# Turning the first tile's query rows and rows with attention by transposing transfers instead of TensorE, with the early orders planned for it

## The chip, the cores and the metric

One core of one Trainium2 chip runs the kernel. The metric is device time in microseconds (us) of one execution, the median of several runs. The core has TensorE (PE; PEld is its weight load), VectorE (DVE), ScalarE (ACT), GpSimd (POOL) and the SyncE queue (SP), which issues all transfers here; the transfers are done by 16 DMA engines.

## The reference

Inputs: `x` of 4 x 1024 x 2048, 64 context keys of 2048 per batch, two gates, a weight of 2048 x 2048 and a bias, all f32.

```
x = x + tanh(g_xattn) * C(layernorm(x))
    C: a = q @ keys^T ; e = softmax(a) ; c = e @ keys
x = x + tanh(g_ffn) * (layernorm(x) @ W^T + bias)
    W = mean(|weight|, per output row) * sign(weight)
```

## The kernel before

The 4096 rows of `x` are 32 tiles of 128 rows. For each tile u:

- **Layernorm 1.** ACT sums the rows and their squares (`sum_rows1`, `square_rows1`; for the first two tiles DVE does it with `ln1_mean`), and POOL makes the scale. `direct_high_q` on ACT then writes the normalised rows as a high f16 part and `low_q` on DVE the f16 rest, both into a slot of `natural`. There are two halves (h = 0, 1) of 1024 columns per tile, and three slots for all that has to be transposed.
- **Turning.** What stands in a `natural` slot has its rows on partitions and has to be transposed for TensorE. Nearly all of it is done by a transposing transfer (`turn_block`, L426, a DMA_TRANSPOSE issued by SP), into `qt` for query rows, `ring_a` or `xn_b` for the rows with attention (called x1). For tile 0 alone, query rows and x1 rows are turned by TensorE in before: `turn_rows` (L2511) multiplies 2 x 8 blocks of 128 x 128 by the identity, part by part, into the two PSUM banks `turn_ps`; then ACT copies one part out and DVE the other (`take_q` L1026 and L1611, `take_x1` L1031 and L1616).
- **Attention.** `scores(u)` (L2553, 32 matmuls of 128 columns), a softmax over 64 keys (`max_logits`, `exp`, `split_probs`, `transpose_probs`, `copy_pt`), four `attend(u, n)` (L2569, two matmuls of 512 columns each), and four times `attention(u, n)` on DVE, which adds the result to the rows.
- **Layernorm 2**, with x1 again in two f16 parts.
- **Product with W.** The signs of the weight are made once, in 16 row blocks w: SP loads a block (`load_w`, four stage buffers), ACT takes signs (`sign`, L1057) and the sum of magnitudes (`sum_abs`, L1063), TensorE turns two blocks at a time (`turn_w(j)`, L2523), ACT and DVE copy them into `wsign` (`take_w(j)`, L1068 and L1754). The row means go through `spread_alpha`, `turn_alpha`, `take_alpha`. Tiles 0 to 3 are multiplied directly: `plain_block(t, n, q)` (L2589, 8 matmuls of 512 columns; q = 0 to 3 make one block of tile t and 512 outputs n). `plain_block(0, n, 0)` waits for both copies of `turn_w(2n+1)`. From tile 4 on, tiles go in 14 pairs through seven half-size products (L2621, `half_product`), with added rows `S1` to `S4`.

All five engines run a list of calls that is written out in the source, so each engine takes its instructions in that order and a late one holds up all behind it. Three tables fix what the lists must agree on: `PE_Q` and `PE_X1` (below which tile TensorE turns), `TURNS` (the order in which TensorE uses the two `turn_ps` banks, which ACT and DVE must have emptied) and `NAT` (the order in which `natural` slots are filled).

The waits that matter for the start:

```
plain_block, q == 0, t == 0:
    pe.wait_ge(out_act, turn("w", 2 * n + 1) + 1)
    pe.wait_ge(out_dve, turn("w", 2 * n + 1) + 1)
turn_w(j):   pe.wait_ge(w_signed, w + 1)      # w = 2j, 2j + 1
             wait_bank(h, "w", j)             # earlier copies out of turn_ps
turn_q:      sp.wait_ge(scores_ready, u)
turn_block:  sp.wait_ge(low_set, i + 1)
sum_rows1:   act.wait_ge(low_set, nat("q", u - 1, 1) + 1)
```

Of the kernel before, what the change touches and what calls it, by code (L numbers as in the profile page):

```python
# [14 lines left out]
def flamingo_gated_kernel(  # L15
# [52 lines left out]
    PE_Q, PE_X1 = 1, 1  # L68
# [3 lines left out]
    TURNS = [("k", 0, 0), ("q", 0, 0), ("q", 0, 1), ("k", 0, 1), ("w", 0, 0), ("w", 1, 0), ("x1", 0, 0),  # L72
              ("w", 2, 0), ("alpha", 0, 0), ("x1", 0, 1), ("w", 3, 0), ("w", 4, 0), ("w", 5, 0), ("alpha", 1, 0),
              ("w", 6, 0), ("w", 7, 0), ("alpha", 2, 0), ("alpha", 3, 0)]
# [82 lines left out]
    with ExitStack() as ctx:  # L157
# [240 lines left out]
        def _(sp):  # L398
# [73 lines left out]
            load_keys(0)  # L472
            load_w(0)
            load_w(1)
            load_gates()
            load_x(1)
            load_x(2)
            load_w(2)
            load_x(3)
            load_w(4)  # L480
            load_w(3)
            load_w(5)
            turn_q(1, 0)
            turn_q(1, 1)
            turn_q(2, 0)
            load_x(4)
            turn_q(2, 1)
            load_w(6)
            load_bias()
            load_w(7)  # L490
            turn_q(3, 0)
            turn_x1(1, 0)
            turn_q(3, 1)
# [4 lines left out]
            turn_q(4, 0)  # L498
            turn_x1(2, 0)
            turn_q(4, 1)  # L500
            turn_x1(2, 1)
            load_w(11)
            load_w(12)
            load_w(13)
            load_w(14)
            load_w(15)
            load_x(5)
# [7 lines left out]
            store(1)  # L515
            store(2)
            load_x(7)
            turn_q(6, 0)
            load_x(8)
            turn_a(0, "A11")  # L520
            turn_q(6, 1)
            turn_a(0, "A12")
            turn_a(0, "S3")
            turn_q(7, 0)
            store(3)
            turn_q(7, 1)
            load_x(9)
            turn_a(0, "S2")
            turn_a(0, "S1")
            turn_a(0, "A22")  # L530
            turn_q(8, 0)
            turn_q(8, 1)
            turn_a(0, "S4")
# [5 lines left out]
            load_x(10)  # L539
            turn_a(1, "S2")  # L540
            turn_q(9, 0)
            turn_q(9, 1)
            store(5)
            turn_a(1, "S1")
            load_x(11)
            turn_q(10, 0)
# [5 lines left out]
            turn_a(2, "A12")  # L552
            store(6)
            turn_q(11, 1)
            load_x(12)
# [63 lines left out]
            store(15)  # L619
            turn_a(6, "S2")  # L620
            turn_a(6, "A22")
            turn_a(6, "S1")
            load_x(21)
# [112 lines left out]
        def _(pool):  # L736
# [83 lines left out]
            mean_1(4)  # L820
            scale1(4)
            scale2(2)
            scale2(3)
            mean_1(5)
            scale1(5)
            scale2(4)
            mean_1(6)
# [6 lines left out]
            reduce_keys(1)  # L834
# [5 lines left out]
            rstd1(10)  # L840
            mean_1(11)
            scale2(8)
# [68 lines left out]
        def _(act):  # L911
# [176 lines left out]

            direct_high_q(0, 0)
            sign(0)  # L1090
            high_keys(0)
            direct_high_q(0, 1)
            tanh_gates()
            sign(1)
            sum_abs(0)
            take_keys(0)
            sum_abs(1)
            take_q(0, 0)
            direct_high_q(1, 0)
            take_q(0, 1)  # L1100
# [3 lines left out]
            sum_abs(2)  # L1104
# [3 lines left out]
            copy_pt(0)  # L1108
            sign(3)
            direct_high_q(2, 0)  # L1110
            sign(4)
            take_w(0)
            direct_high_q(2, 1)
            sign(5)
            exp(1)
            take_w(1)
            direct_high_x1(0, 0)
            copy_pt(1)
            sum_rows1(3)
# [2203 lines left out]
```

## Time and profile before

| what | value |
|---|---|
| runs, median (lowest to highest) | 985.3 us (984.62 to 986.54) |
| the profiled execution's own time | 985.79 us |
| its span, first to last instruction | 984.0 us |
| PE busy | 934.0 us (95%) |
| DVE busy | 840.8 us (85%) |
| ACT busy | 589.3 us (60%) |
| chain that ended last | PE 69%, DVE 10%, issue 7%, ACT 5% |
| mean granted TensorE clock | 0.988 |

A busy share is time in which the engine had an instruction in work, over the span. "Idle before" is the time an engine stood still ahead of an instruction, and "<-" names what it waited for. The chain that ended last is followed back from the last instruction to what released each step. The profiled time is 1.8 us above its span, and 0.5 us above the median.

### The profile page before, as it was taken

Reading aid. Unit: us, or ns where it says so; the run is one execution under the profiler, and the core shown is the slowest. Engines: PE = TensorE matmul, PEld = TensorE weight load, DVE = VectorE, ACT = ScalarE, POOL = GpSimd, SP = SyncE. Lnnn points to the kernel's source line nnn. Section 1 sums busy time; section 2 is a strip of 40 time slices with the busy share of each in tenths; the row PEclk is TensorE's granted clock in tenths of the full one; section 3 lists DMA queues with packets and bytes.
Section 4 is the critical chain, followed back from the end, with each engine's and each line's share of the span. In section 5 each row is a group of like instructions: output and inputs, shape, how many; then the busy total and the mean of one; then the engine's idle time right before and its main releaser. Section 6 shows DMA issues by size and latency. Waiting matters only on the chain.

```text
span 984.0 us, 14349 instructions
## 1 busy us (share of the span) xinstructions
PE 934.0 (95%) x5201; PEld 462.9 (47%) x5201; DVE 840.8 (85%) x1197; ACT 589.3 (60%) x655; POOL 134.9 (14%) x262
## 2 busy tenths in 40 slices
PE   1669999999999999999999999999999999999998
PEld 1445554444444444454444444444444445444443
DVE  6587799897888989899989979998989888889864
ACT  5999973856587573646657364745667464562320
POOL 0011020131001110203111220201102020111000
PEclk9779999999999999999999999999999999999999
DMA  9589747696897988787995959967797967765374
GB/s 332 181 233 229 225 128 199 179 202 112 185 218 154 217 158 221 150 177 168 217 239 97 242 121 237 196 144 202 165 230 125 240 137 152 196 128 102 65 177 186
DMA packets 365141, 178.66 MB, mean 182 GB/s; under 512 B 353424, under 2 KB 353424, under 8 KB 354448
## 3 DMA queue, kind: packets, MB, share of 16 engines
q1 hardware_dynamic: 365072, 177.76, 76.9%
q8 instruction: 41, 0.67, 0.3%
q14 instruction: 28, 0.23, 0.1%
HBM read 55.58 MB, written 33.55 MB: 91 GB/s over the span
## 4 chain that ended last, share of the span: by engine, by line
PE 69%; DVE 10%; issue 7%; ACT 5%; POOL 2%; DMA 2%; SPq 0%; ACTq 0%; DVEq 0%; POOLq 0%
PE y_ps L2621 53%; PE y_ps L2589 7%; PE c_ps L2569 5%; PE s_ps L2553 4%; DVE natural L1571 3%; ACT xn_q L952 1%; DVE xr L1656 1%; DMA xr<-in_x_dram 1%; ACT natural L933 1%; DMA ring_a<-natural 1%; ACT spare L1063 1%; DVE st L1661 1%; DVE snap_a L1689 0%; ACT xn_q L919 0%; DVE xr L1790 0%
## 5 line engine op out<-in xcount | busy, mean ns | idle before, releaser
L2621 PE MATMUL y_ps<-wsign,ring_a 128*128 128x512 fp8e4 x1792 | 400.6, 379 | 2.3 <-DMA ring_a<-natural 1.5
L2621 PEld LDWEIGHTS y_ps<-wsign,ring_a 128*128 128x128 f16 x1792 | 173.9, 98 | 209.8 <-DMA ring_a<-natural 2.8
L2621 PE MATMUL y_ps<-spare,ring_a 128*128 128x512 fp8e4 x896 | 202.8, 379 | 0.7 <-ACT snap_b L1087 0.7
L933 ACT ACTIVATE natural<-xn_a 128x1024 f16<-128x1024 f32 x76 | 79.5, 1053 | 109.2 <-DVE xn_a L1803 49.9
L2621 PEld LDWEIGHTS y_ps<-spare,ring_a 128*128 128x128 f16 x896 | 87.3, 98 | 105.8 <-issue 1.5
L952 ACT ACTIVATE xn_q<-xr,nm,r 128x1024 f32<-128x1024 f32 x62 | 76.8, 1238 | 68.7 <-POOL nm L791 34.3
L1571 DVE TENSOR_TENSOR natural<-xn_a,natural 128x1024 f16<-128x1024 f32 x78 | 94.7, 1216 | 10.9 <-ACT natural L933 10.9
L1571 DVE TENSOR_TENSOR natural<-xn_q,natural 128x1024 f16<-128x1024 f32 x64 | 78.1, 1220 | 25.3 <-ACT natural L933 25.0
L2621 PE MATMUL y_ps<-sg,ring_a 128*128 128x512 fp8e4 x448 | 99.4, 379 | 0.0
L1656 DVE SCALAR_TENSOR_TENSOR xr<-c_ps,coef,xr 128x512 f32<-128x512 f32 x104 | 77.6, 746 | 21.5 <-PE c_ps L2569 21.1
L2569 PE MATMUL c_ps<-kd,pt 128*128 128x512 f16 x256 | 79.7, 394 | 11.5 <-DVE xr L1656 8.6
L2589 PE MATMUL y_ps<-wsign,ring_a 128*128 128x512 fp8e4 x384 | 85.2, 379 | 0.6 <-DVE ring_a L1616 0.6
L1661 DVE BATCH_NORM_STATS2 st<-xr 128x6 f32<-128x512 f32 x104 | 72.2, 694 | 3.6
L1790 DVE TENSOR_TENSOR xr<-xr,bias_b 128x2048 f32<-128x2048 f32 x32 | 72.9, 2281 | 0.0
L784 POOL TENSOR_SCALAR mean<-sum 128x1 f32<-128x1 f32 x30 | 14.7, 489 | 415.9 <-ACT xn_q L919 398.8
L2621 PEld LDWEIGHTS y_ps<-sg,ring_a 128*128 128x128 f16 x448 | 43.6, 98 | 51.8
L927 ACT ACTIVATE xn_q<-xr,mean 128x2048 f16<-128x2048 f32 x30 | 59.9, 1997 | 12.9 <-POOL mean L784 12.7
L919 ACT ACTIVATE xn_q<-xr 128x2048 f16<-128x2048 f32 x30 | 57.2, 1907 | 17.4 <-DMA xr<-in_x_dram 12.0
L2553 PEld LDWEIGHTS s_ps<-kt,qt 128*128 128x128 f16 x1024 | 63.5, 102 | 8.2 <-ACT kt L1019 0.8
L933 ACT ACTIVATE natural<-xn_q 128x1024 f16<-128x1024 f32 x62 | 65.5, 1057 | 2.1 <-DMA qt<-natural 0.2
L2553 PE MATMUL s_ps<-kt,qt 128*128 128x128 f16 x1024 | 66.2, 226 | 0.6 <-ACT kt L1019 0.6
L1703 DVE TENSOR_TENSOR xr<-snap_a,xr 128x512 f32<-128x512 f32 x84 | 58.1, 692 | 2.9
(121 smaller groups left out, 1001.4 us busy)
## 6 DMA issues: line engine op xcount, KB each, us to landing
xr<-in_x_dram SPq DMA_DIRECT2D x32, 1024.0 KB, 6.2
out_dram<-xr SPq DMA_DIRECT2D x30, 1024.0 KB, 5.1
spare<-n_L_ffn_weight_real_dram SPq DMA_DIRECT2D x8, 1024.0 KB, 7.3
ctx_f<-in_ctx_dram SPq DMA_DIRECT2D x8, 512.0 KB, 6.6
xr<-n_L_ffn_weight_real_dram SPq DMA_DIRECT2D x4, 1024.0 KB, 5.0
ctx_f<-n_L_ffn_weight_real_dram SPq DMA_DIRECT2D x4, 1024.0 KB, 7.3
out_dram<-xr SPq DMA_DIRECT2D x8, 256.0 KB, 2.2
ring_a<-natural SPq DMA_TRANSPOSE x102, 4.5
```

What stands on the lines that cost most here:

```text
L927: nc.scalar.activation(junk, xr[:, u % RX, :], ACT.Square, bias=mean1[:, :], accum_out=sq1[:, :]).then_inc(sq1_set, 1)
L933: nc.scalar.activation(natural[:, i % RN, 0, :], src, ACT.Copy).then_inc(high_set, 1)
L952: nc.scalar.activation(xn_q[:, :], xr[:, u % RX, half(h)], ACT.Identity, bias=nm1[:, :], scale=r1[:, :]).then_inc(xn1_set, 1)
L1571: nc.vector.tensor_tensor(natural[:, i % RN, 1, :], src, natural[:, i % RN, 0, :], ALU.subtract).then_inc(low_set, 1)
L1656: nc.vector.scalar_tensor_tensor(out=xr[:, r, chunk(n)], in0=c_ps[:, :], scalar=coef[:, u % 2:u % 2 + 1], in1=xr[:, r, chunk(n)], op0=ALU. ...
L1661: nc.vector.bn_stats(st2[:, n, :], xr[:, r, chunk(n)]).then_inc(stats2, 1)
L1703: nc.vector.tensor_tensor(xr[:, r, chunk(m)], tmp, xr[:, r, chunk(m)], ALU.add).then_inc(y_added, 1)
L1790: nc.vector.tensor_tensor(xr[:, r, :], xr[:, r, :], bias_b[:, :], ALU.add).then_inc(x1b_set, 1)
L2553: last = nc.tensor.matmul(s_ps[:, 0:P], qt[:, k // HALF, part, k % HALF, :], kt[:, k, :], start=(k == 0 and part == 0), stop=(k == ND - 1 ...
L2569: last = nc.tensor.matmul(c_ps[:, :], pt[:, u % 2, :], kd[:, part, chunk(n)], start=(part == 0), stop=(part == 1))
L2589: last = nc.tensor.matmul(y_ps[:, j % 4, :], x1_block(t, k // HALF)[:, part, k % HALF, :], w8[:, k // 2, chunk(n), k % 2], start=(k == 0 a ...
L2621: last = nc.tensor.matmul(y_ps[:, BANKS[j] + n, :], ring_a[:, slot_a(p, j), part, k, :], RIGHT[j][:, k // 2, chunk(n), k % 2], start=(firs ...
```

## The change

Tile 0 is treated like all other tiles: `PE_Q` and `PE_X1` become 0, `turn_rows`, `take_q` and `take_x1` are called no more, and SP issues four more transposing transfers. The lists of all engines are written in another order as far as about tile 12 and at two places near tile 19. Early in the lists, the gates are loaded before the first weight block, `tanh_gates` is ACT's first call, the second tile's `ln1_mean` stands ahead of `low_keys`, and the bias is loaded earlier. Line numbers of the changed kernel are 3 higher on ACT, 1 lower on DVE and SP, 5 lower on PE.

```diff
-    PE_Q, PE_X1 = 1, 1
+    PE_Q, PE_X1 = 0, 0
-    TURNS = [("k", 0, 0), ("q", 0, 0), ("q", 0, 1), ("k", 0, 1), ("w", 0, 0), ("w", 1, 0), ("x1", 0, 0),
-              ("w", 2, 0), ("alpha", 0, 0), ("x1", 0, 1), ("w", 3, 0), ("w", 4, 0), ("w", 5, 0), ("alpha", 1, 0),
+    TURNS = [("k", 0, 0), ("k", 0, 1), ("w", 0, 0), ("w", 1, 0), ("w", 2, 0), ("alpha", 0, 0), ("w", 3, 0),
...
@@ ACT
             copy_pt(0)
+            take_w(0)
+            direct_high_q(2, 0)
+            sum_abs(2)
+            direct_high_q(2, 1)
             sign(3)
...
+            normalise2(1)
+            high_x1(1, 0)
             take_w(1)
...
@@ PE
             turn_maxima()
             turn_keys(0)
-            turn_rows("q", 0, 0)
-            turn_rows("q", 0, 1)
             turn_keys(1)
             scores(0)
...
             scores(1)
-            turn_w(1)
             transpose_probs(1)
             attend(1, 0)
-            turn_rows("x1", 0, 0)
             attend(1, 1)
             attend(1, 2)
             attend(1, 3)
+            turn_w(1)
+            scores(2)
+            transpose_probs(2)
             turn_w(2)
```

**TensorE, from tile 2's attention to the first product of tile 1.** Before (L2511 is the second half of tile 0's x1, L2523 turns weights, L2530 the row means, L2589 is the direct product, x8 for each call):

```order
L2530 MATMUL y_ps<-ident,snap_b 128x128 x4
L2511 MATMUL y_ps<-ident,natural 128x128 x16
L2560 MATMUL s_ps<-ident,prob 128x128
L2589 MATMUL y_ps<-wsign,ring_a 128x512 x24
L2569 MATMUL c_ps<-kd,pt 128x512 x2
L2589 MATMUL y_ps<-wsign,ring_a 128x512 x8
L2569 MATMUL c_ps<-kd,pt 128x512 x2
L2523 MATMUL y_ps<-ident,sg 128x128 x16
L2569 MATMUL c_ps<-kd,pt 128x512 x2
L2553 MATMUL s_ps<-kt,qt 128x128 x32
L2569 MATMUL c_ps<-kd,pt 128x512 x2
L2589 MATMUL y_ps<-wsign,ring_a 128x512 x48
```

Now, the same stretch, from `turn_w(2)` on:

```order
L2518 MATMUL y_ps<-ident,sg 128x128 x16
L2584 MATMUL y_ps<-wsign,ring_a 128x512 x8
L2564 MATMUL c_ps<-kd,pt 128x512 x2
L2584 MATMUL y_ps<-wsign,ring_a 128x512 x8
L2525 MATMUL y_ps<-ident,snap_b 128x128 x4
L2584 MATMUL y_ps<-wsign,ring_a 128x512 x8
L2564 MATMUL c_ps<-kd,pt 128x512 x2
L2584 MATMUL y_ps<-wsign,ring_a 128x512 x8
L2564 MATMUL c_ps<-kd,pt 128x512 x4
L2518 MATMUL y_ps<-ident,sg 128x128 x16
L2548 MATMUL s_ps<-kt,qt 128x128 x32
L2584 MATMUL y_ps<-wsign,ring_a 128x512 x32
```

The transposes of x1 are gone, `turn_w(2)` moved from ahead of `scores(2)` to just ahead of the first product, the row means moved into it, and `turn_w(3)` with `scores(3)` now stand behind all four attentions of tile 2.

**ScalarE, around the copy `take_w(1)` that the first product waits for.** Before (xn_q and natural together are one half of a tile's query rows, sg is a block's signs, ex the exponential):

```order
L952 ACTIVATE xn_q<-xr,nm,r 128x1024
L933 ACTIVATE natural<-xn_q 128x1024
L1057 ACTIVATE sg<-spare 128x8x2x128
L1068 COPY wsign<-y_ps 128x8x128
L952 ACTIVATE xn_q<-xr,nm,r 128x1024
L933 ACTIVATE natural<-xn_q 128x1024
L1057 ACTIVATE sg<-spare 128x8x2x128
L1036 ACTIVATE ex,sum_ex<-logits,neg_max,lscale 128x64
L1068 COPY wsign<-y_ps 128x8x128
```

Now, ending at the same copy:

```order
L1060 ACTIVATE sg<-spare 128x8x2x128
L930 ACTIVATE xn_q,sq1<-xr,mean1 128x2048
L941 ACTIVATE natural<-xr,nm2,r2 128x1024
L1060 ACTIVATE sg<-spare 128x8x2x128
L1066 ACTIVATE spare,abs_sum<-spare 128x2048
L955 ACTIVATE xn_q<-xr,nm1,r1 128x1024
L936 ACTIVATE natural<-xn_q 128x1024
L1039 ACTIVATE ex,sum_ex<-logits,neg_max,lscale 128x64
L1001 ACTIVATE xn_a<-xr,nm2,r2 128x2048
L936 ACTIVATE natural<-xn_a 128x1024
L1071 COPY wsign<-y_ps 128x8x128
```

Before, this copy follows the exponential of tile 1; now it follows that of tile 2, tile 1's second normalisation, a half of tile 3's queries and five magnitude sums (blocks 0 to 4).

**The SP queue at the start.** Before:

```order
L405 DMA xr<-in_x_dram 128x2048
L414 DMA ctx_f<-in_ctx_dram 64x2048 x2
L435 DMA spare<-in_L_ffn_weight_real_dram 128x2048 x2
L438 DMA gates<-in_g_xattn_dram 128x1
L439 DMA gates<-in_g_ffn_dram 128x1
L405 DMA xr<-in_x_dram 128x2048 x2
L435 DMA xr<-in_L_ffn_weight_real_dram 128x2048
L405 DMA xr<-in_x_dram 128x2048
L435 DMA spare<-in_L_ffn_weight_real_dram 128x2048
L435 DMA ctx_f<-in_L_ffn_weight_real_dram 128x2048
L435 DMA spare<-in_L_ffn_weight_real_dram 128x2048
L426 DMA_TRANSPOSE qt<-natural 128x16x128 x3
```

Now, from the first weight block on:

```order
L434 DMA spare<-in_L0_ffn_weight_real_dram 128x2048
L404 DMA xr<-in_x_dram 128x2048
L434 DMA spare<-in_L0_ffn_weight_real_dram 128x2048
L434 DMA xr<-in_L0_ffn_weight_real_dram 128x2048
L425 DMA_TRANSPOSE qt<-natural 128x16x128
L404 DMA xr<-in_x_dram 128x2048
L425 DMA_TRANSPOSE qt<-natural 128x16x128
L441 DMA bias_b<-in_L0_ffn_bias_dram 128x2048
L404 DMA xr<-in_x_dram 128x2048
L425 DMA_TRANSPOSE qt<-natural 128x16x128
```

The two transposing transfers of tile 0's queries now stand between loads, so that tiles 2 and 3, the bias and the later weight blocks are issued only after the waits of these transfers.

## Rows read from the trace of the kernel before

**Rows 1.** The profile's page, busy time by engine and one group of DVE.

```profile
PE 934.0 (95%) x5201; PEld 462.9 (47%) x5201; DVE 840.8 (85%) x1197; ACT 589.3 (60%) x655; POOL 134.9 (14%) x262
...
L1656 DVE SCALAR_TENSOR_TENSOR xr<-c_ps,coef,xr 128x512 f32<-128x512 f32 x104 | 77.6, 746 | 21.5 <-PE c_ps L2569 21.1
```

**Rows 2.** Busy time by stage: stretch, length, engines' busy us, clock, DMA share, GB/s.

```profile
0.00:80.00 80.00, 41.53 (x312) 28.29 (x313) 53.73 (x95) 66.07 (x66) 8.05 (x33) 0.85 0.80 246
...
200.00:300.00 100.00, 97.50 (x572) 48.78 (x571) 84.23 (x130) 67.92 (x84) 14.63 (x28) 1.00 0.81 175
```

**Rows 3.** Timeline of PE: start, length, instruction, idle before it and its releaser.

```profile
31.91 3.57 PE L2553 MATMUL s_ps<-kt,qt 128*128 128x128 f16 x32 [0.56 <-ACT kt L1019]
...
40.20 1.03 PE L2569 MATMUL c_ps<-kd,pt 128*128 128x512 f16 x2 [1.40 <-ACT pt L1043]
...
71.61 5.34 PE L2589 MATMUL y_ps<-wsign,ring_a 128*128 128x512 fp8e4 x24 [0.58 <-DVE ring_a L1616]
76.79 0.59 PE L2569 MATMUL c_ps<-kd,pt 128*128 128x512 f16 x2
...
80.83 1.95 PE L2553 MATMUL s_ps<-kt,qt 128*128 128x128 f16 x32
...
83.05 10.52 PE L2589 MATMUL y_ps<-wsign,ring_a 128*128 128x512 fp8e4 x48
...
152.35 0.66 PE L2530 MATMUL y_ps<-ident,snap_b 128*128 128x128 f32 x4 [0.64 <-DVE snap_b L1762]
```

**Rows 4.** Groups by line and shape, 0 to 80 us: what the change removes.

```profile
L2511 PE MATMUL y_ps<-ident,natural 128*128 128x128 f16 x64 | 6.7, 287 | 4.3 <-ACT kt L1019 2.2 <-DVE alpha_b L1768 1.2 <-ACT qt L1026 0.9
...
L1026 ACT COPY qt<-y_ps 128x1024 f16<-128x1024 f16 x2 | 2.0, 994 | 0.0
L1031 ACT COPY ring_a<-y_ps 128x1024 f16<-128x1024 f16 x2 | 2.0, 990 | 0.0
...
L1611 DVE COPY qt<-y_ps 128x1024 f16<-128x1024 f16 x2 | 1.4, 693 | 2.3 <-PE y_ps L2511 2.3
L1616 DVE COPY ring_a<-y_ps 128x1024 f16<-128x1024 f16 x2 | 1.4, 681 | 0.0
```

**Rows 5.** The query tile `qt`, 0 to 75 us: landing of its transposing transfers.

```profile
DMA to landing us min/median/max: 4.3/4.6/5.7
```

**Rows 6.** Timeline of DVE: second half of tile 0's queries, then tile 1's statistics.

```profile
20.19 1.23 DVE L1571 TENSOR_TENSOR natural<-xn_q,natural 128x1024 f16<-128x1024 f32 x1
...
21.67 2.46 DVE L1563 BATCH_NORM_STATS2 st<-xr 128x6 f32<-128x512 f32 x4
```

**Rows 7.** Timeline of ACT, 66 to 82 us: one of each kind.

```profile
66.93 2.09 ACT L998 ACTIVATE xn_a<-xr,nm,r 128x2048 f32<-128x2048 f32 x1 [1.14 <-POOL nm L780]
68.94 0.42 ACT L1036 ACTIVATE ex<-logits,neg_max,lscale 128x64 f32<-128x64 f32 x1
...
71.20 0.26 ACT L1043 COPY pt<-s_ps 128x128 f16<-128x128 f16 x1
71.36 1.25 ACT L952 ACTIVATE xn_q<-xr,nm,r 128x1024 f32<-128x1024 f32 x1
72.63 1.06 ACT L933 ACTIVATE natural<-xn_q 128x1024 f16<-128x1024 f32 x1
...
76.34 1.90 ACT L1057 ACTIVATE sg<-ctx_f 128x2048 fp8e4<-128x2048 f32 x1
78.14 1.89 ACT L919 ACTIVATE xn_q<-xr 128x2048 f16<-128x2048 f32 x1
...
80.04 1.89 ACT L1063 ACTIVATE spare<-spare 128x2048 f32<-128x2048 f32 x1
...
81.93 1.99 ACT L927 ACTIVATE xn_q<-xr,mean 128x2048 f16<-128x2048 f32 x1
```

**Rows 8.** Busy time by 5 us, columns as in rows 2: the granted clock at the start.

```profile
35.00:40.00 5.00, 1.88 (x22) 1.57 (x20) 1.51 (x9) 5.00 (x9) 0.25 (x1) 0.93 0.71 133
40.00:45.00 5.00, 3.10 (x6) 0.39 (x6) 2.89 (x4) 4.97 (x5) 0.95 (x3) 0.50 0.42 78
```

More of the change, by code:

```diff
@@ L1166, in _ @@
             sum_abs(14)
+            take_w(6)
             sign(15)
-            take_w(6)
+            take_w(7)
+            sum_rows1(5)
+            exp(4)
+            square_rows1(5)
             sum_abs(15)
-            sum_rows1(5)
-            take_w(7)
-            square_rows1(5)
+            copy_pt(4)
             normalise2(3)
@@ L1860, in _ @@
             attention(0, 1)
+            low_q(2, 0)
             attention(0, 2)
-            spread_alpha(0)
-            low_q(2, 0)
+            attention(0, 3)
+            low_q(2, 1)
             take_w(0)
-            attention(0, 3)
             max_logits(1)
+            scale_bias()
+            split_probs(1)
             rows_x1(0)
-            split_probs(1)
-            low_q(2, 1)
+            attention(1, 0)
+            attention(1, 1)
+            low_x1(0, 0)
+            attention(1, 2)
@@ L1897, in _ @@
+            low_x1(2, 0)
             add_bias(0)
-            split_probs(3)
+            low_x1(2, 1)
+            add_bias(1)
+            spread_alpha(5)
+            add_bias(2)
+            attention(3, 0)
+            spread_alpha(6)
             finish_y(0, 0)
-            spread_alpha(4)
+            take_w(4)
+            spread_alpha(7)
+            take_w(5)
             low_q(4, 0)
-            low_x1(2, 0)
+            attention(3, 1)
+            finish_y(1, 0)
             low_q(4, 1)
-            attention(3, 0)
@@ L1905, in _ @@
-            low_x1(2, 1)
-            attention(3, 1)
-            add_bias(1)
+            take_alpha(1)
+            spread_alpha(8)
+            spread_alpha(9)
+            finish_y(0, 1)
             attention(3, 2)
-            spread_alpha(5)
+            spread_alpha(10)
+            finish_y(1, 1)
+            finish_y(2, 0)
+            make_t1(0)
+            take_w(6)
+            make_t2(0)
+            attention(3, 3)
             max_logits(4)
             split_probs(4)
-            spread_alpha(6)
@@ L1943, in _ @@
             spread_alpha(14)
+            take_alpha(2)
+            finish_y(2, 1)
             spread_alpha(15)
+            attention(4, 0)
+            low_q(5, 0)
             finish_y(0, 2)
+            finish_y(1, 2)
+            attention(4, 1)
+            low_x1(3, 0)
             low_q(5, 1)
+            key_max(1)
+            finish_y(2, 2)
             take_alpha(3)
-            finish_y(1, 2)
-            finish_y(2, 2)
+            finish_y(0, 3)
             low_x1(3, 1)
-            finish_y(0, 3)
-            make_t1(1)
+            make_n4(0)
+            attention(4, 2)
             max_logits(5)
+            attention(4, 3)
             split_probs(5)
@@ L2216, in _ @@
             make_s4(6)
+            add_bias(17)
+            attention(18, 0)
+            attention(18, 1)
+            low_a(6, "A22")
             attention(18, 2)
@@ L2676, in _ @@
             attend(3, 0)
+            turn_w(4)
             plain_block(1, 1, 1)
             plain_block(1, 1, 2)
+            plain_block(1, 1, 3)
+            turn_w(5)
             attend(3, 1)
[L2680 to L2683 removed]
             plain_block(2, 0, 0)
             plain_block(2, 0, 1)
[L2686 to L2702 removed]
+            plain_block(2, 0, 2)
+            turn_alpha(1)
+            plain_block(2, 0, 3)
+            attend(3, 2)
+            plain_block(2, 1, 0)
+            plain_block(2, 1, 1)
+            plain_block(2, 1, 2)
+            plain_block(2, 1, 3)
+            turn_w(6)
+            plain_block(0, 2, 0)
+            plain_block(0, 2, 1)
+            attend(3, 3)
             plain_block(0, 2, 2)
+            scores(4)
+            turn_w(7)
             plain_block(0, 2, 3)
@@ L2735, in _ @@
             plain_block(3, 0, 2)
+            plain_block(3, 0, 3)
             attend(5, 3)
-            plain_block(3, 0, 3)
             plain_block(3, 1, 0)
@@ L2818, in _ @@
             half_product(1, 4, 0, 1)
-            scores(10)
             attend(9, 3)
@@ L2822, in _ @@
             half_product(1, 4, 1, 1)
+            scores(10)
             half_product(1, 5, 0, 0)
@@ L2834, in _ @@
             half_product(2, 0, 1, 0)
[L2835 removed]
+            scores(11)
+            attend(10, 1)
             half_product(2, 0, 1, 1)
             half_product(2, 1, 0, 0)
[L2838 to L2839 removed]
             half_product(2, 1, 0, 1)
@@ L2991, in _ @@
             half_product(5, 6, 1, 1)
+            scores(19)
+            transpose_probs(19)
             half_product(6, 0, 0, 0)
@@ L2994, in _ @@
             half_product(6, 0, 0, 1)
-            scores(19)
             attend(18, 1)
```

487 lines of the change are left out of this document (211 added, 276 removed), and 12 rows, old and new, of the table NAT.

## The prediction

> **What bounds the kernel now.** I read the busy times first: PE 934.0 of 984.0 us [rows 1], so the time is TensorE's work plus the 50 us in which it has none. The stages say where these lie: in the first 80 us PE is busy for 41.5, so 38.5 of the 50 are lost there, while ACT is busy for 66.1 of 80 [rows 2]. Of ACT's 14 idle us most lie ahead of the first rows' statistics, so in the rest of that stretch it hardly rests: the start is ACT's. Third, PE's own timeline: the first product of a tile with the weight starts at 71.61, that of tile 1 at 83.05 [rows 3], and behind it PE runs dense, with one wait of 0.64 at 152.35 for the last row means, which hang on ACT's last magnitude sums. The end therefore moves with two things: how much work PE has done by the time it runs dense, and the few waits after that.
>
> **What the change removes.** On PE 64 transposes, 6.7 us; on ACT four copies of 0.99, 4.0 us; on DVE four copies of 0.69, 2.7 us [rows 4]. PE's 6.7 us lie in the stretch in which it waits for others, mostly beside that waiting; they are worth at most what ACT and DVE let through. ACT's 4.0 us are the real offer. In their place stand four transposing transfers, 4.3 to 5.7 us from issue to landing [rows 5].
>
> **First scores.** They start at 31.91 behind ACT's second copy of keys [rows 3]. The calls on ACT ahead of that copy are the same as before, less two copies of 0.99 (the gates' tanh and `sum_abs(0)` only change places). So the copy comes 2.0 earlier, and the scores at 29.9. The second half of tile 0's queries must have landed by then. DVE finished it at 20.19 + 1.23 = 21.4; now `ln1_mean(1)`, whose statistics took 2.46 with another 0.3 to join them [rows 6], and the gates' 0.4 stand ahead of it: 24.6. With 4.6 us of landing that is 29.2. It just fits. At the bounds of [rows 5] the scores start between 29.9 and 30.4, if no load is in the way. I take 29.9: a gain of 2.0 so far.
>
> **From there to the first product: ACT's list.** `plain_block(0, 0, 0)` needs `take_w(1)` on ACT. In the new order that copy stands behind tile 2's exponential and a half of tile 3's queries. From the end of the key copy, 29.8 by the step above, ACT has ahead of it: three signs, three magnitude sums and two row sums (8 x 1.90 = 15.2), two squares (4.0), four query halves (1.25 + 1.06 each, 9.2), two halves of x1 at 1.25 (2.5), three exponentials with their read-out (about 0.6 each, 1.8), two copies of probabilities (0.5), the normalisation of tile 1 (2.1) and one high half (1.0), and two copies of weights at 0.99, the price of a copy of this shape [rows 4], 2.0. That is 38.3 [rows 7]: 68.1 if ACT never waits.
>
> It will wait. The sum over tile 2's rows waits for DVE's low half of q(1, 1) (1.23 [rows 6]): 1.3. The sum over tile 3's rows waits for q(2, 1)'s low half, which stands on DVE behind the last attention of tile 0: 0.7. Tile 2's exponential waits for its scores. DVE's four attentions of tile 1 (0.75 each [rows 1] and the statistics behind them) now have the two low halves of x1 between them, which eats the 2.0 us won above, so the scores come where they were, ending near 67: 1.7. Another 1.0 goes into smaller waits for POOL. Sum 4.7: `take_w(1)` is done at **72.8**. By the bounds (no wait, or twice these) it is 68.1 to 77.5; rows for these waits exist before only one by one, so I take the middle. `turn_w(2)` must follow that copy, having no bank before it, and the first product starts at about 74, against 71.61.
>
> **The next gate: sign(7).** PE's list puts `turn_w(3)` and `scores(3)` ahead of tile 1's product, and `turn_w(3)` needs the signs of block 7. Before, ACT had them at 76.34 + 1.90 = 78.2 [rows 7]. Now there stand between `take_w(1)` and that point: a magnitude sum, a copy of probabilities, a query half, a copy of weights, a high half, a sign, a row sum and the sign itself, 1.9 + 0.3 + 2.3 + 1.0 + 1.0 + 1.9 + 1.9 + 1.9 = 12.2. So the signs are ready at 85.0. With 0.5 for the second half of `turn_w(3)` and 1.95 for the scores [rows 3], tile 1's product starts at 87.4. Up to that start both orders have done the same work on PE, apart from the 64 transposes. So this is the lag: 87.4 - 83.05 = **4.3 us**.
>
> The mechanism in one sentence: the four copies are gone, but three magnitude sums and one row sum (7.6 us) were moved ahead of block 7's signs, and the sums had not been urgent.
>
> **After it.** Tile 3's probabilities hang on ACT: 1.9 + 1.0 + 2.0 + 2.1 + 1.9 to the exponential, another 1.2 to the probabilities, 95.1. PE finishes tile 1's 32 matmuls (10.52 x 32 / 48 = 7.0 [rows 3]) at 94.4: **0.7** more. Then PE is dense; ACT's remaining signs and copies come 0.7 to 2 us ahead of need, so nothing is won back there. The 0.64 at 152.35 goes, because the last magnitude sum is some 14 us ahead of the last row means: **-0.6**.
>
> **Sum.** 985.8 + 4.3 + 0.7 - 0.6 = 990.2 for an execution like the profiled one, which stood 0.5 above the median: **989.7 us**, slower by 0.4%. About 0.2%, 2 us, is what a measurement here can tell from no change.
>
> **A place where a rule and the rows part.** With its transposes gone, PE has next to no work from about 67 to 72.8. In the profile the granted clock was 0.93 of its full 2.4 GHz over 35 to 40 us, where PE was busy for 1.88 of 5, and 0.50 (1.2 GHz) over the next 5 [rows 8]; there a pair of 512-column matmuls took 1.03, and later 0.59 [rows 3], 0.22 more for each matmul. If the clock falls in the new hole, the first eight to sixteen matmuls of the product lose 1.8 to 3.5 us. But PE would stand ready for `turn_w(3)` at about 82.7, 2.3 ahead of block 7's signs, so I cost it at 0; what is left over at the upper end is 1.2. The Trainium skill, "TensorE: Matmul & The Clock Gate", section "HAM oscillation", warns of exactly such idle gaps, behind which TensorE starts at half rate; taken at its full price that would make the sum 990.9 instead of 989.7.
>
> **Rivals.**
> *Faster: ACT's relief gets through.* If my waits of 4.7 are not there and DVE is not the pace of tile 1's attention, the start moves by the 4.0 us of copies: 985.8 - 4.0 - 0.5 = 981.3. For it: ACT is the bound, and 4.0 us of its work are gone. Against: the list of ACT as it stands puts 7.6 us of sums ahead of what PE waits for. It decides at block 7's signs: before 76 it wins. Chance 0.18.
> *No change: the lag is paid back.* Between 200 and 300 us PE loses 2.5 us [rows 2] to rows and snapshots that come late. A PE that arrives 4 us later finds them ready, and the new orders reach that far: 989.7 - 2.5 = 987.2, and with a lag of 2 to 3 us 985 to 986. Against: tile 4's attention now comes some 25 us later, into that very stretch. Chance 0.19.
> *Slower still: DVE.* It is 84% busy from 200 to 300 [rows 2]. Tile 4's four attentions (0.75 each [rows 1], about twice that with the statistics) now run beside the last direct products. If they don't fit, the first pair's rows come late and 4 us are added: 994. A first query half held up behind loads would give much the same, 993. Chance 0.10.
>
> **How the numbers follow.** The forecast, with its own range of 987.3 to 992.5 (lag 2 to 7), has 0.53. The range 983.0 to 995.0 leaves out most of the faster case and the far end of the slow ones, about 0.2. Faster by over 0.2% (below 983.3): 0.18. Within: 0.19. Slower: 0.63.
>
> **What would show it.** PE's timeline: first scores near 30, first product (L2584) near 74, tile 1's product near 87; ACT's sign of block 7 ending near 85; no wait at the last row means. The view of waits should name ACT's copy or sign ahead of `turn_w(2)` and `turn_w(3)`. I am wrong if block 7's signs end before 79, if the waits after 200 us shrink by more than 2 us, or if PE waits for a transposing transfer ahead of the first scores or the first product.

## The result and the profile after

The changed kernel takes **996.9 us** (median of 3 runs, 995.69 to 999.41) against 985.3 before: a ratio of 1.012, 95% interval 1.0093 to 1.0147. It is slower, as forecast, but by 11.6 us and not by 4.4; the time lies above the range. The profiled execution took 999.4 us with a span of 997.6; it is the longest of the three, 2.5 above the median, so what follows adds up to about 2 us more than was measured.

The profile's page of the changed kernel, busy time by engine:

```profile
span 997.6 us, 14202 instructions
## 1 busy us (share of the span) xinstructions
PE 933.3 (94%) x5137; PEld 459.6 (46%) x5137; DVE 838.5 (84%) x1193; ACT 586.0 (59%) x651; POOL 134.0 (13%) x262
```

All engines have a little less to do than in [rows 1], ACT and DVE by the copies that were removed. PE's work is only 0.7 us less, though 6.7 us of transposes are gone: the instructions that are left take 6.0 us more, and PE's idle time grew by 14.3. The span is 13.6 us longer. The view of stages says where (stretch, length, busy us of each engine, granted clock, share and rate of DMA):

```profile
0.00:80.00 80.00, 34.91 (x223) 22.56 (x224) 48.16 (x88) 63.38 (x64) 12.49 (x33) 0.79 1.00 263
...
200.00:300.00 100.00, 100.00 (x563) 49.32 (x561) 84.99 (x123) 68.25 (x83) 14.88 (x25) 1.00 0.86 187
300.00:997.60 697.60, 679.67 (x3668) 327.98 (x3665) 602.62 (x849) 363.92 (x417) 89.42 (x176) 1.00 0.76 170
```

Against [rows 2], the first 80 us have 6.6 us less of PE's work, the size of the removed transposes, though by then the two lists do not stand at the same call; from 200 to 300 us PE no longer rests, where it had lost 2.5; and behind 300 us, where I had expected nothing, it idles for 17.9 us (before 8.4).

PE's timeline of the changed kernel at the start (columns as in rows 3; L2518 turns weights, L2548 are scores, L2584 is the direct product):

```profile
30.08 3.60 PE L2548 MATMUL s_ps<-kt,qt 128*128 128x128 f16 x32 [3.94 <-ACT kt L1022]
...
71.92 1.86 PE L2518 MATMUL y_ps<-ident,sg 128*128 128x128 f16 x16 [3.38 <-ACT wsign L1071]
73.58 3.06 PE L2584 MATMUL y_ps<-wsign,ring_a 128*128 128x512 fp8e4 x8
...
84.97 0.60 PE L2564 MATMUL c_ps<-kd,pt 128*128 128x512 f16 x2 [0.85 <-DVE xr L1655]
85.41 1.06 PE L2518 MATMUL y_ps<-ident,sg 128*128 128x128 f16 x16
86.31 1.95 PE L2548 MATMUL s_ps<-kt,qt 128*128 128x128 f16 x32
88.09 4.26 PE L2584 MATMUL y_ps<-wsign,ring_a 128*128 128x512 fp8e4 x19
```

and two lines of ACT's:

```profile
70.67 0.99 ACT L1071 COPY wsign<-y_ps 128x1024 f16<-128x1024 f16 x1
...
81.40 1.90 ACT L1060 ACTIVATE sg<-ctx_f 128x2048 fp8e4<-128x2048 f32 x1
```

As far as block 7's signs this is the walk of the prediction: scores at 30.08 (29.9 forecast), `take_w(1)` done at 71.7 (72.8), block 7's signs at 83.3 (85.0). Tile 1's product starts at 88.1 (87.4) against 83.05 in [rows 3], a lag of **5.0 us**, but the signs are not what it waits for: `turn_w(3)` starts 2.1 us after them, behind PE's waits for DVE.

The rest of the 13.6 us can be followed at the scores of each tile. From tile 12 to 18, and from 20 on, both PE lists have done the same work by then, so the difference of their start times is the lag:

| scores of tile | 12 | 15 to 18 | 20, 21 | 22 to 24 | 25 to 31 |
|---|---|---|---|---|---|
| before, us | 353.5 | 435.2 and on | 582.8 and on | 636.2 and on | 730.6 and on |
| lag of the changed kernel, us | 1.2 | 2.3 | **11.2** | 13.1 | 13.7 |

So of 5.0 us, 3.9 are paid back by tile 12, and 8.9 are lost at one place, between the scores of tiles 18 and 20. PE there, in the changed kernel (L2616 is a half-size product, L2555 turns probabilities):

```profile
544.42 1.95 PE L2548 MATMUL s_ps<-kt,qt 128*128 128x128 f16 x32 [0.84 <-issue]
552.81 0.29 PE L2555 MATMUL s_ps<-ident,prob 128*128 128x128 f16 x1 [6.45 <-DVE prob L1635]
552.91 3.60 PE L2616 MATMUL y_ps<-wsign,ring_a 128*128 128x512 fp8e4 x8
556.30 1.05 PE L2564 MATMUL c_ps<-kd,pt 128*128 128x512 f16 x2
```

and in the kernel before (L2569 is an attention product, L2560 turns probabilities):

```profile
545.03 1.95 PE L2553 MATMUL s_ps<-kt,qt 128*128 128x128 f16 x32
546.82 0.59 PE L2569 MATMUL c_ps<-kd,pt 128*128 128x512 f16 x2
547.25 3.62 PE L2621 MATMUL y_ps<-wsign,ring_a 128*128 128x512 fp8e4 x16
550.71 0.59 PE L2569 MATMUL c_ps<-kd,pt 128*128 128x512 f16 x2
551.14 3.62 PE L2621 MATMUL y_ps<-wsign,ring_a 128*128 128x512 fp8e4 x16
554.59 0.22 PE L2560 MATMUL s_ps<-ident,prob 128*128 128x128 f16 x1
```

Before, 8 us of products stand between tile 19's scores and the transpose of its probabilities. Now nothing does, and PE waits 6.45 us for DVE's probabilities, and 0.84 ahead of the scores; behind the hole eight matmuls and an attention pair ran at half pace (3.60 against 1.89, 1.05 against 0.59). From the scores of tile 18 to those of tile 20 the view of stretches has, before and changed:

```profile
525.49:582.76 57.27, 55.66 (x307) 27.11 (x306) 51.22 (x72) 30.16 (x35) 11.84 (x19) 1.00 0.78 175
```

```profile
527.76:593.95 66.19, 58.32 (x307) 27.52 (x306) 51.68 (x72) 30.36 (x35) 9.39 (x19) 0.95 0.69 151
```

The same 307 instructions of PE, with 7.87 us of idle time instead of 1.61 and 2.66 us more of work: 8.9. DVE meanwhile, in the changed kernel:

```profile
546.10 1.22 DVE L1570 TENSOR_TENSOR natural<-xn_a,natural 128x1024 f16<-128x1024 f32 x1
547.35 1.23 DVE L1802 TENSOR_TENSOR xn_a<-xn_b,xn_a 128x1024 f32<-128x1024 f32 x1
549.70 1.23 DVE L1570 TENSOR_TENSOR natural<-xn_a,natural 128x1024 f16<-128x1024 f32 x1 [1.12 <-ACT natural L936]
550.84 0.28 DVE L1620 TENSOR_REDUCE logits<-s_ps 128x64 f32<-128x128 f32 x1
...
552.53 0.22 DVE L1635 SCALAR_TENSOR_TENSOR prob<-ex,prob 128x64 f16<-128x64 f32 x1
...
556.13 2.29 DVE L1789 TENSOR_TENSOR xr<-xr,bias_b 128x2048 f32<-128x2048 f32 x1
558.33 0.75 DVE L1655 SCALAR_TENSOR_TENSOR xr<-c_ps,coef,xr 128x512 f32<-128x512 f32 x1
```

The scores are ready at 546.4; DVE looks at them at 550.8, when three subtractions for the next pair of tiles (one of which waits 1.12 for ACT) are through. So 4.5 of the 6.45 us are other calls in DVE's list, and 2.0 are the softmax itself.

### The profile page after: what moved, and what is told of

Same layout as the page of the kernel before. It is cut to its first block, busy times and chain, and to the rows that moved or that the text cites. A ratio compares the mean times of both kernels' runs of the same rounds, so it can differ in the third digit from the quotient of the medians.

```text
span 997.6 us, 14202 instructions
## 1 busy us (share of the span) xinstructions
PE 933.3 (94%) x5137; PEld 459.6 (46%) x5137; DVE 838.5 (84%) x1193; ACT 586.0 (59%) x651; POOL 134.0 (13%) x262
## 4 chain that ended last, share of the span: by engine, by line
PE 73%; DVE 9%; issue 7%; ACT 3%; DMA 2%; POOL 1%; SPq 1%; ACTq 0%; DVEq 0%; POOLq 0%
PE y_ps L2616 52%; PE y_ps L2584 11%; PE c_ps L2564 5%; PE s_ps L2548 4%; DVE natural L1570 3%; DMA ring_a<-natural 1%; DVE xr L1655 1%; ACT xn_q L955 1%; ACT natural L936 1%; SPq L425 1%; DMA xr<-in_x_dram 1%; PE y_ps L2518 1%; DVE snap_a L1688 0%; ACT xn_q L922 0%; DVE xr L1789 0%
## 5 line engine op out<-in xcount | busy, mean ns | idle before, releaser
L2616 PE MATMUL y_ps<-wsign,ring_a 128*128 128x512 fp8e4 x1792 | 402.5, 380 | 2.3 <-DVE snap_a L1688 1.9
L2616 PEld LDWEIGHTS y_ps<-wsign,ring_a 128*128 128x128 f16 x1792 | 174.3, 98 | 210.8 <-issue 3.1
L2616 PE MATMUL y_ps<-spare,ring_a 128*128 128x512 fp8e4 x896 | 202.6, 379 | 0.0
L2616 PEld LDWEIGHTS y_ps<-spare,ring_a 128*128 128x128 f16 x896 | 87.4, 98 | 104.7
L2616 PE MATMUL y_ps<-sg,ring_a 128*128 128x512 fp8e4 x448 | 99.4, 379 | 0.0
L2584 PE MATMUL y_ps<-wsign,ring_a 128*128 128x512 fp8e4 x384 | 86.9, 383 | 0.0
L787 POOL TENSOR_SCALAR mean<-sum 128x1 f32<-128x1 f32 x30 | 17.6, 586 | 431.1 <-ACT xn_q L922 413.2
L2548 PE MATMUL s_ps<-kt,qt 128*128 128x128 f16 x1024 | 66.9, 227 | 5.7 <-ACT kt L1022 3.9
L2548 PEld LDWEIGHTS s_ps<-kt,qt 128*128 128x128 f16 x1024 | 63.9, 102 | 13.7 <-ACT kt L1022 4.2
L930 ACT ACTIVATE xn_q<-xr,mean 128x2048 f16<-128x2048 f32 x30 | 60.0, 1999 | 13.8 <-POOL mean L787 13.6
L2616 PEld LDWEIGHTS y_ps<-sg,ring_a 128*128 128x128 f16 x448 | 43.6, 98 | 51.5
L922 ACT ACTIVATE xn_q<-xr 128x2048 f16<-128x2048 f32 x30 | 57.2, 1908 | 14.9 <-DMA xr<-in_x_dram 11.5
```

The lines of the kernel that those rows point to most:

```text
L930: nc.scalar.activation(junk, xr[:, u % RX, :], ACT.Square, bias=mean1[:, :], accum_out=sq1[:, :]).then_inc(sq1_set, 1)
L2548: last = nc.tensor.matmul(s_ps[:, 0:P], qt[:, k // HALF, part, k % HALF, :], kt[:, k, :], start=(k == 0 and part == 0), stop=(k == ND - 1 ...
L2584: last = nc.tensor.matmul(y_ps[:, j % 4, :], x1_block(t, k // HALF)[:, part, k % HALF, :], w8[:, k // 2, chunk(n), k % 2], start=(k == 0 a ...
L2616: last = nc.tensor.matmul(y_ps[:, BANKS[j] + n, :], ring_a[:, slot_a(p, j), part, k, :], RIGHT[j][:, k // 2, chunk(n), k % 2], start=(firs ...
```

## The experiments

Twelve kernels, in three questions: which edit costs what, what makes the place at tile 19 dear, and where the rest goes. Ratios are to the kernel before as timed beside each group of runs (medians of 985.4 to 986.2), so runs of different groups are compared by their ratios.

**1. Tile 19's lists undone, all else as changed.** On PE (and SP, ACT and DVE likewise):

```diff
             half_product(5, 6, 1, 1)
-            scores(19)
-            transpose_probs(19)
             half_product(6, 0, 0, 0)
             attend(18, 0)
             half_product(6, 0, 0, 1)
+            scores(19)
             attend(18, 1)
...
             attend(18, 2)
...
+            transpose_probs(19)
```

> The changed kernel, with the lists around tile 19 (on PE, ACT, DVE and SP) as they were before. Theory A (the loss is made at tile 19, where PE's list puts the transpose of tile 19's probabilities straight behind its scores): 986.5 to 988.5 us, PE's wait ahead of that transpose gone from the view of waits, the scores of tile 20 on within 3 us of the kernel before. Theory B (the start's 5 us lag is what costs, and tile 19's wait is only where a late DVE shows): 990 or more.

988.99 us (987.31 to 989.48), ratio 1.0031 (1.0018 to 1.0044): 0.5 above theory A's range and short of B's. PE's wait ahead of the transpose is gone, and the lag is 1.6 at tile 20, but 3.7 from tile 25 on, where theory A allowed 3. The other way round:

**2. The kernel before with tile 19's lists alone.**

> The kernel before, with the lists around tile 19 alone as the change has them; tile 0 is still turned by TensorE. Theory A: 993 to 996 us, with a wait of some 6 us on PE ahead of the transpose of tile 19's probabilities and the clock at half behind it. Theory B: within 1.5 us of 985.3.

994.83 us (994.37 to 995.86), ratio 1.0095 (1.008 to 1.011). PE waits 6.17 for tile 19's probabilities, and the lag steps from 1.0 to 10.0 us between tiles 18 and 20. So the reordered lists at tile 19 cost about 9.2 us by themselves and all the rest 3.4; their sum, 12.6, is near the 11.6 measured.

**3. Tile 19 undone on PE and ACT alone**, DVE and SP as changed.

> The changed kernel, with tile 19's place undone on PE and ACT alone; DVE still does the softmax of tile 19 ahead of the attentions of tile 18. Theory A in its narrow form (it is PE's list that waits): within 1.5 us of the run with all lists undone. Rival (DVE's order is the loss: tile 18's attentions come late, and with them the pair they belong to): 3 us or more above that run.

998.73 us, ratio 1.0132 (1.0117 to 1.0147): nothing won, and 9.7 above run 1, as the rival had it. PE in this kernel:

```profile
544.72 1.95 PE L2548 MATMUL s_ps<-kt,qt 128*128 128x128 f16 x32
556.56 1.03 PE L2564 MATMUL c_ps<-kd,pt 128*128 128x512 f16 x2 [9.89 <-DVE xr L1655]
```

The wait moved to `attend(18, 1)`, which needs a PSUM bank that DVE empties in `attention(18, 0)`, and DVE's changed list does that only behind the softmax of tile 19 and two bias additions. So PE's order alone is not the cause: DVE's order stands behind both waits. (DVE's old order under PE's new one was not run; the two lists would wait for each other: PE's `attend(18, 0)` stands behind the transpose of tile 19's probabilities, and DVE makes these only behind `attention(18, 0)`.)

**4. The softmax of tile 19 moved up** on DVE, and the exponential on ACT, in the changed kernel:

```diff
             low_a(6, "A12")
+            max_logits(19)
+            split_probs(19)
             finish_pair(5, "C12", 1)
             low_a(6, "S3")
             make_s2(6)
             low_a(6, "S2")
-            max_logits(19)
-            split_probs(19)
```

> The changed kernel with VectorE's softmax of tile 19 (and ScalarE's exp) moved up, ahead of the low halves S3 and S2 of block row 6; the two bias adds stay ahead of tile 18's attentions. Theory A (TensorE's wait of 6.4 us is only the late softmax): that wait falls to 3 us or less and the time to 989 to 991.5. Theory B (the whole stretch of VectorE's list up to attention(18,0) counts): the wait falls as well, but one of 2 to 5 us comes at attend(18,1), which waits for attention(18,0), and the time is 992 to 996.

1000.76 us, ratio 1.0149 (1.0135 to 1.0162): about 2.9 slower than the changed kernel by the ratios. PE:

```profile
547.68 0.23 PE L2555 MATMUL s_ps<-ident,prob 128*128 128x128 f16 x1 [2.01 <-DVE prob L1635]
547.78 1.89 PE L2616 MATMUL y_ps<-wsign,ring_a 128*128 128x512 fp8e4 x8
...
560.07 1.03 PE L2564 MATMUL c_ps<-kd,pt 128*128 128x512 f16 x2 [8.25 <-DVE xr L1655]
```

Theory B held in kind and was too small in size: the wait for the softmax fell to 2.0, 8.25 came at `attend(18, 1)`, where it had 2 to 5, and the time is above its 992 to 996.

**5. The attentions of tile 18 moved up as well**, ahead of the two bias additions:

```diff
+            attention(18, 0)
+            make_s4(6)
+            attention(18, 1)
             add_bias(16)
-            make_s4(6)
-            add_bias(17)
-            attention(18, 0)
-            attention(18, 1)
             low_a(6, "A22")
+            add_bias(17)
```

> The kernel with the softmax of tile 19 moved up, and with attention(18,0) and attention(18,1) ahead of the two bias adds as well; TensorE's list stays as changed. Theory (VectorE's order against TensorE's sets the loss at tile 19): both waits together at most 3 us, time 988.5 to 991. Rival (TensorE's early scores(19) and transpose of its probabilities cost the 8 us whatever VectorE does): 994 or more.

992.41 us (991.98 to 994.21), ratio 1.0071 (1.0057 to 1.0084): by the ratios 4.8 us are back with PE's list left as changed, and in the trace the loss between the scores of tiles 18 and 20 falls from 8.9 to 5.0. The two waits were to be at most 3 us and are 4.7, and the time lies between the ranges of theory and rival:

```profile
548.36 0.23 PE L2555 MATMUL s_ps<-ident,prob 128*128 128x128 f16 x1 [2.02 <-DVE prob L1635]
...
555.21 0.60 PE L2564 MATMUL c_ps<-kd,pt 128*128 128x512 f16 x2 [2.71 <-DVE xr L1655]
```

So DVE's order accounts for about half. That the other half lies with PE's own list, which leaves nothing between scores and the transpose, is argued: no run moved the transpose alone back behind the products.

**6. Only the turning of tile 0 changed**, all lists in the order of before.

> The kernel before, with tile 0 turned by transfers and nothing else in the lists moved: eight calls on ACT and DVE and four on PE go, four transfers are put into SP's list where their rows are ready. Theory C (transfers in TensorE's place cost nothing by themselves, and ACT's four copies are a gain that the new lists give away): first scores at 30 to 31, first product at 68 to 71, total 982.5 to 985.5. Rival (a transfer is late and takes the place of the copies): first scores after 33 or the first product after 73, total 987 or more.

989.72 us (988.59 to 991.37), ratio 1.0047 (1.003 to 1.0064): slower by 4.1, and the range of the theory is missed. The rival's time came without its signs: the first scores start at 30.8, the first product at 71.1. PE in this kernel:

```profile
68.91 0.23 PE L2556 MATMUL s_ps<-ident,prob 128*128 128x128 f16 x1 [2.60 <-DVE prob L1636]
71.06 7.02 PE L2585 MATMUL y_ps<-wsign,ring_a 128*128 128x512 fp8e4 x24 [1.91 <-DMA ring_a<-natural]
77.91 0.59 PE L2565 MATMUL c_ps<-kd,pt 128*128 128x512 f16 x2
```

The first product starts no later than in [rows 3], but its 24 matmuls take 7.02 instead of 5.34. It waits for the second half of x1. DVE has these rows ready at 58.5, and they land at 71.0: 3.2 us pass ahead of the transfer, which stands on SP behind another transfer, a weight block and the bias, and its issue takes 7.1:

```profile
57.62 2.90 SPq L426 DMA_TRANSPOSE ring_a<-natural  x1
60.61 0.53 SPq L435 DMA_DIRECT2D xr<-n_L_ffn_weight_real_dram  x1
61.19 0.42 SPq L442 DMA_DIRECT2D bias_b<-in_L_ffn_bias_dram  x1
61.67 7.11 SPq L426 DMA_TRANSPOSE ring_a<-natural  x1
```

**7 and 8. The two halves of that, apart**: x1 alone by transfers, and the queries alone.

```diff
-    PE_Q, PE_X1 = 1, 1
+    PE_Q, PE_X1 = 1, 0
```

> Before's lists, with the rows with attention of tile 0 (x1) alone turned by transfers; its queries stay with TensorE. Theory (the late landing of x1 and the half clock behind the hole it leaves make the loss of the transfers-only kernel, 989.7): first product at 70 to 72 us with 24 matmuls in 6 us or more, time 988 to 990.5. Rival (the two query transfers, 10.8 us long and ahead of the sign loads, make it): first product no later than 71 with its 24 matmuls in at most 5.6 us, time 985 to 986.5.

990.31 us, ratio 1.0051 (1.0035 to 1.0067); the first product at 72.23 with 7.03 us. As the theory had it in time, with the product 0.2 us later than its range. In the trace only 2.2 us of the lag are there at tile 12; 4.4 more come near 430 us, where POOL takes up tile 15's statistics at 415.3 instead of 410.5 (see 10). That execution took 993.8 us, 3.5 above the median, so most executions lose less there.

```diff
-    PE_Q, PE_X1 = 1, 1
+    PE_Q, PE_X1 = 0, 1
```

> Before's lists, with the queries of tile 0 alone turned by transfers; its rows with attention stay with TensorE. With the x1-only kernel at 4 us over the kernel before and its first product at half clock (7.0 us for 24 matmuls), the x1 transfer looks like the whole of the loss. Theory (the queries' transfers cost nothing by themselves, since scores(0) begin a little earlier and the sign loads are not yet needed): first product at 69 to 72 us with 24 matmuls in under 6 us, time 984.5 to 986.5. Rival (the sign loads held back to 28 us delay the sign blocks and the first product): 987 or more.

985.77 us, ratio 1.0003 (0.9993 to 1.0012). The queries' transfers cost nothing and bring a lead of 2.2 us by tile 12, which is gone again by tile 22. So the loss of 6 is made by x1's transfers. PE in this kernel, where it still turns x1:

```profile
67.46 1.05 PE L2509 MATMUL y_ps<-ident,natural 128*128 128x128 f16 x16 [1.19 <-DVE alpha_b L1768]
68.87 0.23 PE L2558 MATMUL s_ps<-ident,prob 128*128 128x128 f16 x1 [0.35 <-DVE prob L1636]
69.96 5.34 PE L2587 MATMUL y_ps<-wsign,ring_a 128*128 128x512 fp8e4 x24 [0.86 <-ACT ring_a L1033]
```

**9. The start's order mended**: the kernel of 1, with ACT's `take_w(1)` right behind tile 1's probabilities, sums moved behind the signs, and PE's `turn_w(2)` ahead of tile 2's scores; DVE's `take_w(1)`, PE's `turn_w(1)` and SP's `load_w(7)` stand earlier as well. On ACT:

```diff
             copy_pt(1)
+            take_w(1)
             sign(4)
...
+            direct_high_q(3, 0)
             sum_abs(4)
-            direct_high_q(3, 0)
...
-            take_w(1)
-            sum_abs(5)
+            take_w(2)
             copy_pt(2)
             direct_high_q(3, 1)
-            take_w(2)
+            sign(6)
             high_x1(1, 1)
-            sign(6)
+            sign(7)
+            sum_abs(5)
             sum_rows1(4)
-            sign(7)
+            take_w(3)
             sum_abs(6)
-            take_w(3)
```

> The kernel with tile 19's lists undone (989.0), and with the sign rows of blocks 1 to 3 turned and copied earlier: ScalarE copies block 1 right behind tile 1's probabilities, and sums and signs stand in another order; TensorE turns block 2 before tile 2's scores. Theory A (the start lag of 5 us is carried to the end): tile 1's product at 82.5 to 85 instead of 88.1, time 984 to 986.5. Rival B (the lag is paid back by tile 12, where the undone kernel is only 0.5 us behind, and its 3.2 us are lost in the later waits near 430, 630 and 720 us): the product comes earlier and the time stays at 988 to 989.5. Rival C (another engine holds the start): tile 1's product at 87 us or later.

988.16 us (986.99 to 989.56), ratio 1.0022 (1.0013 to 1.0031). Tile 1's product starts at 85.4, against 87.4 in the kernel of 1, and at tile 12 this kernel is 0.65 us *ahead* of before; yet at tile 25 it lags by 3.5. Rival B: 1.35 are lost near 430, 1.9 near 630, 0.95 near 714 us. At the start it is now x1's transfer that PE waits for, 1.95 us ahead of the first product at 69.4.

**10 and 11. Who takes it there.** The first two places follow GpSimd's maximum over the partitions for the keys of the next batch. POOL in the kernel of 9:

```profile
403.15 0.38 POOL L798 PARTITION_ALL_REDUCE kmax_all<-kmax  x1 [7.13 <-issue]
410.77 0.26 POOL L787 TENSOR_SCALAR mean<-sum 128x1 f32<-128x1 f32 x1 [7.25 <-issue]
...
414.60 0.19 POOL L794 TENSOR_TENSOR nm<-mean,r 128x1 f32<-128x1 f32 x1
```

The row sum of tile 15 that `mean` needs is there at 405.6, but POOL takes it up at 410.8. ACT waits 3.83 for it, DVE then 3.47 for ACT, and PE 1.58 for DVE:

```profile
430.61 1.89 PE L2616 MATMUL y_ps<-wsign,ring_a 128*128 128x512 fp8e4 x8 [1.58 <-DVE snap_a L1688]
```

The edit moves the maxima of batches 2 and 3 behind the statistics of tiles 15 and 23, and DVE's key scales of batch 2 behind the softmax of tile 15:

```diff
@@ POOL
             scale2(12)
-            reduce_keys(2)
             mean_1(15)
             rstd1(15)
             scale2(13)
+            reduce_keys(2)
...
-            reduce_keys(3)
             mean_1(22)
...
             rstd1(23)
+            reduce_keys(3)
@@ DVE
             attention(13, 2)
-            key_scales(2)
...
             split_probs(15)
+            key_scales(2)
```

Made in the kernel of 9:

> The start-order kernel (988.2), with GpSimd's maximum over the partitions for key batches 2 and 3 moved behind the statistics of tiles 15 and 23, and VectorE's key scales of batch 2 behind the softmax of tile 15. Theory (of its lag at the end of 3.5 us, 1.35 near 430 and 1.9 near 630 us come from GpSimd, which is held 7 to 11 us by that maximum while the row means of tiles 15 and 22 stand behind it): both steps go, the lag behind the kernel before at tile 22's scores is under 0.5 us, time 984.5 to 986. Rival (VectorE is full there and any place serves the wait again a little later): lag at the end 2.5 us or more, time 987.5 to 989.

984.93 us (983.57 to 986.66), ratio 0.9992 (0.9983 to 1.0001). Both steps are gone: the lag is -0.65 from tile 15 to 24. POOL now:

```profile
406.07 0.23 POOL L787 TENSOR_SCALAR mean<-sum 128x1 f32<-128x1 f32 x1 [9.65 <-ACT xn_q L922]
```

Near 630 us only POOL's list was changed, so that step went by the maximum alone; near 430 the key scales moved too, and the two are not told apart.

In the kernel before, alone:

> The kernel before with the same move of GpSimd's maxima and VectorE's key scales, nothing else. Theory: before only lost some 0.7 us to these two places (waits of 0.24 and 0.46 us), so 984.5 to 986. Rival (the move opens a new wait where the maximum now stands): 987 or more, and then the start-order kernel gains nothing by it either.

984.97 us, ratio 0.9995 (0.9986 to 1.0004): a lead of 0.8 us in the trace from tile 15 on, too little to measure.

**12. The two parts that helped, together**: queries by transfers (8) and the maxima later (11), in the lists of before.

> Before's lists with the queries of tile 0 turned by transfers and GpSimd's maxima moved as in the run before: the two parts that helped, together. Theory (the query transfers alone bring a lead of 2.2 us by tile 12, of which the two places of GpSimd's maximum take back 1.1 near 430 and 1.2 near 630 us): the lead stays, 2 to 3 us at tile 22's scores, time 982.3 to 984. Rival (the lead is used up again wherever TensorE meets VectorE next): 984.5 to 986, no different from the kernel before.

983.79 us (983.43 to 985.85), ratio **0.9981 (0.9972 to 0.999)**, against 985.4 before: the shortest time of the study, if by 0.2%. The lead of 2.06 us stays from tile 21 to the end.

## Why the prediction was wrong

**The step that failed is one it doesn't have.** The part on the change names two places near tile 19 where the lists are written in another order; the prediction costs the start and says of the rest that PE is dense, though 11.5 of its 50 idle us in the kernel before lie behind 80 us. No term, no rival and no bound covers them, though the list shows scores and the transpose of their probabilities back to back, with a softmax on another engine between them. Runs 1 and 2 put 9.2 us there. The forecast 989.7 is within 0.7 of the kernel in which only that was undone, 988.99, but by luck, as the next two points say. The place could have been costed from the trace of before: from the end of tile 19's scores at 546.98 DVE takes 5.4 us to the probabilities, and the products that lay beside it were taken away.

```profile
552.17 0.23 DVE L1636 SCALAR_TENSOR_TENSOR prob<-ex,prob 128x64 f16<-128x64 f32 x1
```

**The lag of 4.3 + 0.7 at the start: near in size, by another gate.** It measured 5.0. ACT's part was walked well: its waits ahead of `take_w(1)` add up to 4.6 us against 4.7, and the copy came 1.1, block 7's signs 1.7 earlier than walked. But the signs did not hold tile 1's product: PE's waits for tile 2's attention on DVE (0.40 and 0.85) stand directly ahead of `turn_w(3)`, which starts at 85.41, 2.1 after the signs. The 0.7 at tile 3's probabilities did not appear. So two misses made up for each other. The sentence on the mechanism also counts one sum too many: the lists move two magnitude sums (blocks 4 and 5) and one row sum ahead of block 7's signs, 5.7 us and not 7.6; the walk itself has the right calls.

**That the lag reaches the end: wrong.** The rival "the lag is paid back" was the truer mechanism, and a sign that the prediction had named against itself came in part: the waits from 200 to 300 us shrank by 2.5, over its 2, while those behind 300 grew by 9.6. Between tile 1's product and tile 12's scores PE idled 3.1 us before (270.45 us with 267.32 busy) and not at all after (266.59 of 266.59): 2.5 from 200 to 300 us, as the rival said, and the 0.64 of the row means. With 0.7 less of busy time these make the 3.9. That run 1 still came out near the forecast is luck: its lag is 0.5 at tile 12 and 3.7 from tile 25 on, so 3.2 us were lost again at waits that the prediction did not look at. Run 9 shows how little the start decides: 2.0 us won there, 0.8 at the end, which the intervals of the two runs do not tell from nothing.

**The clock, costed at 0: it cost 1.2.** The eight matmuls behind the wait for `turn_w(2)` took 3.06 instead of 1.89, and the granted clock from 70 to 74 us was 0.50, half of 2.4 GHz. I expected the loss to vanish in a wait of 2.3 ahead of block 7's signs; that wait did not exist. By the waits of the trace the 1.2 us pass into the lag: the row means stand behind these matmuls on PE, DVE's L1761 waits for them, and DVE then runs without a pause to the attention that PE waits for ahead of `turn_w(3)`.

```profile
79.34 0.28 DVE L1761 TENSOR_SCALAR snap_b<-ones,abs_sum 128x128 f32<-128x128 f32 x1 [2.07 <-PE y_ps L2525]
```

The Trainium skill, "TensorE: Matmul & The Clock Gate", section "HAM oscillation", says that a wait between two blocks of matmuls can throttle TensorE, so that the next block starts at half rate. The trace agrees: 3.06 against 1.89 us here, and more dearly 3.60 against 1.89 behind the wait at tile 19. In run 6 the first product took 7.02 against 5.34, with a granted clock of 0.69 from 72 to 76 us. In run 8 the 16 transposes that TensorE still does at 67.46 lie in that hole, the clock stays at 1.00 from 66 to 74, and the product takes 5.34; the wait of 1.91 for x1's transfer is gone there too, so what the transposes do by themselves is not told apart.

**What stays open.** Why the POOL maximum holds its engine for 7 us in one kernel and 8.7 in another was not tried (POOL's spans are rough in such a profile), nor was the step of 0.95 near 714 us, where PE waits 0.78 for a transfer of rows and which run 10 keeps (0.87). Why the issue of x1's second half took 7.1 us in run 6 is open too. The changed kernel with the maxima moved was not run; whether it would win the 3 us of run 10 is not shown.

## What to carry to other kernels

Where every engine follows a written list, read the whole difference of the lists, and cost each place where a producer and its consumer came closer together: the round trip through the other engines (here scores, softmax, transpose: 6.45 us with the work that DVE had ahead of it) has to be covered by work in the waiting engine's own list. Move such an order on all engines together; moving it on one only moves the wait. And in a kernel that is 95% busy on one engine, lost time at the start can be paid back from later slack (3.9 of 5.0 us here), while a long instruction on a nearly idle engine, with statistics queued behind it, can set the pace hundreds of microseconds later (3.2 us in run 9).

## What was not expected of the hardware

- GpSimd's maximum over 128 partitions of one column is shown as 0.4 to 1.2 us, but the next instruction of that engine came 7.2 to 8.7 us after its start near 405 us and 11 to 12 near 610 us (606.92 to 617.99 before), and the profile shows nothing that it waited for.
- TensorE's granted clock fell in holes of the steady part too: 0.53 from 550 to 556 us, where PE was busy for 3.19 of 6, and eight matmuls cost 3.60 instead of 1.89.
- A transposing transfer of one half took SP 2.9 us to issue in run 6, and the next, which stood behind a weight block and the bias, 7.1.
